# Last batch of a Mamba and mixture-of-experts layer in blocks of 512 tokens, with feed-forward parts spread anew

## The reference

```
h = layernorm(x) * (1 + ca) + sa
x = x + ga * mamba(h)
h = layernorm(x) * (1 + cb) + sb
x = x + gb * ffn(h)

mamba(h):                       # 512 channels, 16 states per channel
    val, gate = split(h @ W_in)
    val = silu(conv3(val))      # along the tokens, centred
    B, C = val @ W_B, val @ W_C
    Delta = softplus((val @ W_delta + delta_base) @ W_tau)
    dA = Delta[..., None] * -exp(A_log)
    A_bar = exp(dA);  B_bar = expm1(dA) / (dA + 1e-6) * Delta * B
    h_t = A_bar_t * h_{t-1} + B_bar_t * val_t          # the scan along 2048 tokens
    y_t = sum over the states of h_t * C_t
    return (y * silu(gate)) @ W_out + h

ffn(h):                         # 8 experts and a shared one, hidden size 256
    scores = sigmoid(h @ gate_W);  the two best experts, weights normalised
    return sum over experts of weight_e * (gelu(h @ W1_e + b1_e) @ W2_e + b2_e)
           + gelu(h @ Ws1 + bs1) @ Ws2 + bs2
```

## Time and profile before

| | |
|---|---|
| median of three runs | 5074.86 us |
| profiled execution | 5076.93 us |
| its span, first to last instruction | 5075.1 us |
| busy: TensorE, VectorE, ScalarE, GpSimd | 3917.0, 4160.2, 3989.1, 3740.0 us |
| mean granted TensorE clock | 0.867 |
| DMA | 1104.28 MB, mean 218 GB/s |

### The profile page before, as it was taken

One profiled execution on the slowest core, in us unless ns is written; L12 is line 12 of the kernel. 1 busy time (PEld: TensorE's weight loads), 2 busy tenths in 40 slices (PEclk: granted clock), 3 DMA queues, 4 the chain that ended last, 5 costly groups with the idle time before them and its releaser, 6 DMA issues.

```text
span 5075.1 us, 36705 instructions
## 1 busy us (share of the span) xinstructions
PE 3917.0 (77%) x9708; PEld 1636.1 (32%) x9708; DVE 4160.2 (82%) x3798; ACT 3989.1 (79%) x4187; POOL 3740.0 (74%) x2292
## 2 busy tenths in 40 slices
PE   6441242888888988888898888898888876778989
PEld 3210010333333333333333333333333323333443
DVE  1277899989899999999898989999999989998110
ACT  2386788898899898988898988889899887887111
POOL 0189997787888887887888887888888797888101
PEclk8775565899999999898999999899999887879989
DMA  4589887788888888888888888888888887777322
GB/s 133 140 270 272 256 232 201 216 237 232 231 257 216 260 237 231 227 234 234 229 240 228 257 217 256 228 242 224 230 255 223 225 226 201 220 206 217 101 91 74
DMA packets 365658, 1104.28 MB, mean 218 GB/s; under 512 B 42501, under 2 KB 45445, under 8 KB 358150
## 3 DMA queue, kind: packets, MB, share of 16 engines
q1 hardware_dynamic: 274314, 799.91, 45.7%
q0 software_dynamic: 91136, 302.03, 30.9%
HBM read 673.29 MB, written 160.06 MB: 164 GB/s over the span
## 4 chain that ended last, share of the span: by engine, by line
PE 17%; issue 17%; ACT 17%; DMA 17%; POOL 16%; DVE 13%; SPq 0%; POOLq 0%; DVEq 0%; ACTq 0%
DMA ysum<-hs 12%; PE ps L1024 5%; PE ps L1040 5%; POOL inv L1302 4%; POOL hs L1279 4%; ACT inv L680 3%; DVE ps L1072 3%; DVE ps L1078 3%; PE ps L994 2%; DVE ps L1085 2%; ACT inv L675 2%; POOL ysum L1289 2%; ACT th L687 1%; ACT inv L685 1%; POOL hid L1319 1%
## 5 line engine op out<-in xcount | busy, mean ns | idle before, releaser
L1302 POOL TENSOR_TENSOR inv<-inv,th 128x1024 f32<-128x1024 f32 x512 | 1279.0, 2498 | 263.7 <-ACT th L687 262.9
L1279 POOL TENSOR_TENSOR hs<-hs,Cb 128x1024 f32<-128x1024 f32 x512 | 1296.7, 2533 | 91.8 <-DVE hs L1102 69.9
L1024 PE MATMUL ps<-hf,w1r 128*128 128x512 f32 x2304 | 1139.8, 649 | 55.0 <-ACT xn L760 30.4
L1051 PE MATMUL ps<-Brow,pick 48*128 48x512 bf16 x1024 | 355.1, 431 | 780.9 <-DVE hs L1102 776.1
L1040 PE MATMUL ps<-w2r,hid 128*128 128x512 f32 x1792 | 833.5, 612 | 1.1 <-issue 1.1
L687 ACT ACTIVATE th<-delta,halfA 128x1024 f32<-128x1024 f32 x512 | 582.7, 1138 | 231.4 <-POOL inv L1302 231.1
L1072 DVE TENSOR_TENSOR ps<-ps,us 128x1024 f32<-128x1024 f32 x512 | 627.7, 1226 | 116.9 <-PE ps L1051 116.6
L1289 POOL DMA_DIRECT2D ysum<-hs x480 | 446.8, 931 | 328.1 <-DMA ysum<-hs 290.5
L1085 DVE SCALAR_TENSOR_TENSOR ps<-ps,coef,inv 128x1024 f32<-128x1024 f32 x512 | 658.2, 1286 | 31.6 <-POOL inv L1302 9.7
L1024 PEld LDWEIGHTS ps<-hf,w1r 128*128 128x128 f32 x2304 | 463.2, 208 | 654.9 <-issue 596.9
L1092 DVE SCALAR_TENSOR_TENSOR ps<-nrd,inv_kappa,ps 128x1024 f32<-128x1024 f32 x512 | 659.0, 1287 | 15.0
(11 more groups left out here) (157 smaller groups left out, 5139.8 us busy)
## 6 DMA issues: line engine op xcount, KB each, us to landing
Cb<-c_rows SPq DMA_DIRECT2D x512, 512.0 KB, 4.7
ysum<-hs POOLq DMA_DIRECT2D x512, 512.0 KB, 5.6
w2r<-w_scaled SPq DMA_DIRECT2D x144, 512.0 KB, 7.0
w1r<-in_W SPq DMA_DIRECT2D x144, 512.0 KB, 6.0
gbc<-expert_gates SPq DMA_DIRECT2D x128, 256.0 KB, 5.5
aw<-in_W_val SPq DMA_DIRECT2D x64, 256.0 KB, 5.1
xa<-in_x SPq DMA_DIRECT2D x32, 512.0 KB, 6.3
h_residual<-hT SPq DMA_DIRECT2D x16, 1024.0 KB, 7.3
```

The source lines that it names most:

```text
L1024: mm = t.matmul(o, w1r[:, n % 2, k, h * P:(h + 1) * P], hf[:, k, :], start=(k == 0), stop=(k == G - 1))
L1279: gp_.tensor_tensor(hs[:, c % 3, :], hs[:, c % 3, :], Cb[:, c % 2, :], ALU.mult).then_inc(hC_done, 1)
L1302: gp_.tensor_tensor(inv[:, c % 6, :], inv[:, c % 6, :], th[:, c % 2, :], ALU.mult).then_inc(thinv_done, 1)
```

## The change

For the first three batches nothing changes but the layout in DRAM. For the last batch a unit is now two channel groups side by side over 512 tokens, 2 x 512 columns, so that a block of 512 tokens takes two units; y of block 12 is whole after unit 25, of 13 after unit 27, of 14 after unit 29, of 15 after unit 31. Instructions that take a constant of the channel are issued once for each half (`for cols, g in parts(u)`): Square, Tanh, the second Exp, times_weight, times_ratio, the scan, and the Ln of inverse_delta.

Slots and steps are taken apart. PACE maps slots to steps: up to slot 383 one step to a slot as before; slots 384 to 511 take the 160 steps of windows 12 to 16; slots 512 to 575 those of windows 17 and 18. ScalarE's places are mapped in the same proportion by share_act. All rows in DRAM lie by blocks of 512. In SyncE's order, the DMAs of the scan (C, unit, u, B, y) stand ahead of the steps' and the gate load and a block's first unit load behind them.

```
-    NK = NQ // 2
-    NU = NK * G
+    NU = NQ * G // 2
...
-    c_d = dram("c_rows", [NK, N, TB])
-    delta_d = dram("delta_rows", [NK, G, P, TB])
+    c_d = dram("c_rows", [NQ, N, T])
+    delta_d = dram("delta_rows", [NQ, G, P, T])
...
+        SIZES = [2] * 6 + [1] * 4
...
+        def rows_of(d, u):
+            (q, n), i = BLOCKS[BLOCK_OF[u]], u - FIRST_U[BLOCK_OF[u]]
+            return (d[q:q + 2, i] if n == 2 else d[q, 2 * i:2 * i + 2]).rearrange("h p t -> p h t")
+
+        def parts(u):
+            n, i = BLOCKS[BLOCK_OF[u]][1], u - FIRST_U[BLOCK_OF[u]]
+            return [(slice(0, TB), i)] if n == 2 else [(slice(0, T), 2 * i), (slice(T, TB), 2 * i + 1)]
...
+        PACE = [(-3 * WIN, 0, -3 * WIN, 0), (0, 2 * WIN, 0, 2 * WIN), (2 * WIN, (NQ - 4) * WIN, 2 * WIN, (NQ - 4) * WIN), ((NQ - 4) * WIN, NQ * WIN, (NQ - 4) * WIN, (NQ + 1) * WIN), (NQ * WIN, (NQ + 2) * WIN, (NQ + 1) * WIN, (NQ + 3) * WIN)]
+        SLOTS = range(PACE[0][0], PACE[-1][1])
+
+        def share(t):
+            for t0, t1, v0, v1 in PACE:
+                if t0 <= t < t1:
+                    j, n, m = t - t0, t1 - t0, v1 - v0
+                    return range(v0 + j * m // n, v0 + (j + 1) * m // n)
...
-                sp.wait_ge(gy_st, 16 * G * (k + 1))
+                sp.wait_ge(gy_st, 16 * units_before_end(qf))
...
+                row = c_d[q:q + 2, n, :] if fronts(u) == q + 2 else c_d[q, n:n + 1, :].broadcast_to([2, T])
+                sp.dma_start(halves(Cb[:, (c + 1) % 2, :]), row.partition_broadcast(P)).then_inc(C_ld[(c + 1) % 2], 16)
...
-                s.activation(th[:, c % 2, :], delta[:, u % 2, :], ACT.Tanh,
-                             scale=halfA[:, c % N, u % G:u % G + 1]).then_inc(th_done, 1)
+                for cols, g in parts(u):
+                    ins = s.activation(th[:, c % 2, cols], delta[:, u % 2, cols], ACT.Tanh, scale=halfA[:, c % N, g:g + 1])
+                ins.then_inc(th_done, 1)
...
+                for cols, g in parts(u):
+                    ins = v.tensor_tensor_scan(hs[:, c % 3, cols], abar[:, c % 4, cols], X(c)[:, cols],
+                                               0.0 if begins(u) else carry[:, g, c % N:c % N + 1], ALU.mult, ALU.add)
+                ins.then_inc(scan_done, 1)
+
+            times_weight(c)
+            for H, r in steps_of(c)[:1]:
+                dve_steps(dve, H, r, True)
+            times_ratio(c)
+            times_u(c + 1)
+            scan(c)
+            times_abar(c + 1)
+            for i, (H, r) in enumerate(steps_of(c)):
+                if i:
+                    dve_steps(dve, H, r, True)
+                dve_steps(dve, H, r)
...
-                for H in WINDOWS:
-                    for r in range(WIN):
-                        pe_slot(pe, H, r)
+                for t in SLOTS:
+                    pe_slot(pe, t)
+                    for H, r in steps_of(t):
+                        pe_steps(pe, H, r)
```

More of the change, by code:

```diff
@@ new lines, in at @@
+            def at(place):
+                if batch % 4 == 1 and place in ("logs", 0):
+                    inverse_delta(4 * batch // N + 1, place)
+                for i in share_act(NP * batch + PLACES.index(place)):
+                    b, j = divmod(i, NP)
+                    act_steps(act, *divmod(b, WIN // 4), PLACES[j])
+            at("start")
+            for c in states[0:2]:
+                square(c)
+            at("half squared")
+            for c in states[2:4]:
+                square(c)
@@ L883, in pe_jobs @@
+            if w == 7:
+                if place == "start":
+                    take_t(qn, (2, 3))
+                    gelu(qf, 2)
         def pe_jobs(H, r):
```

572 lines of the change are left out of this document (306 added, 266 removed).

## The result

| | before | after |
|---|---|---|
| median | 5075.2 us (5061.0 to 5090.0, 4 runs) | 5204.0 us (5194.5 to 5210.4, 4 runs) |
| ratio, 95% interval | | 1.0252 (1.0219 to 1.0285) |
| profiled execution, span | 5076.9, 5075.1 us | 5194.5, 5192.6 us |
| first scan to scan of state 384 | 3343.5 us | 3457.8 us (+114.3) |
| from there to the end of the last scan | 1054.8 us | 1235.4 us (+180.6) |

The account below looks back on a forecast made before the run. VectorE was taken to bound the slots and TensorE alone the stretch behind the last scan. 5075.1 + 145.7 (last 128 slots) - 176.1 (behind them) = 5044.7, forecast as 5045 us, range 4970 to 5105.

Parts of the forecast that it names:

- Behind the last scan: Stretch after the last scan: only block 15's feed-forward part is left there, 390.0 to 213.9 us, a term of -176.1.
- (a), the pieces: DRAM rows by 512 tokens, loads in 2 KB instead of 4 KB pieces: taken as nothing, at most 10 us over the run.
- (b), SyncE's order: SyncE's reordered DMA queue: each DMA waits for things done a window earlier, the C load has a slot of slack; nothing.
- The last 128 slots: From scan 384 to the last: 1054.8 us plus part, cuts and TensorE waits becomes 1200.5, a term of +145.7.
- The cuts: Three VectorE instructions per state halved in the last 128 slots, 384 more: 45 us, bounds 0 to 77.
- The fifth part: One more feed-forward part in the last 128 slots: 14 us of VectorE work and 87 of further waits.
- the dearer bound: VectorE's wait for B in the last 128 slots: 133 us if each TensorE product is 5% longer; 110 was taken.
- Where the lateness stands: 21 of 32 double slots have too much TensorE work; named: 491, 411, 403, 415, 423, 475, 499 and 503.
- The clock: TensorE's granted clock in the last 128 slots: near 0.94, as in window 12 before, keeping waits near the lower price.
- Rival 3: Hand-overs between ScalarE and TensorE come late, 80 us on top of 1200 in the last 128 slots: 5125; chance 0.13.
- Rival 2: Time lost in the last 128 slots, 1256 us and more, eats the 176 gained: 5075 to 5100; chance 0.18.
- marks set for "wrong": Halved pair over 0.2 us dearer, VectorE waiting over 10 us for ScalarE or GpSimd, first 384 slots over 3640 us.

Follow-up runs that it names:

- b_c2k: The kernel before with only the rows of C in DRAM by 512 tokens (2 KB pieces): 5190.0 us, 1.0222.
- b_lnwait: The kernel before with only a block's first load of delta moved to the end of step 19 and waiting for both halves of the log's sum: 5116.5 us, 1.0088.
- a_cuts: a_4k_ln with one step to a slot, halved instructions kept, block 14's part behind the last scan again: 5125.7 us, 1.0094.
- a_4k_ln: The changed kernel with 4 KB rows for blocks 0 to 11 and each load of delta waiting only for the half it reads: 5085.6 us, 1.0030.
- a_bal2_c1: a_c1 with double slots light for TensorE and not close together between a load's issue and its use: 5044.9 us, 0.9944.
- a_c1: a_4k_ln with C loaded once per short block and multiplied into both halves: 5068.3 us, 0.9989.

## Why the prediction was wrong, by its steps

**Behind the last scan: right.** -176.1 said, -178.6 measured.

**"Edits at nothing", (a), the pieces: this step failed.** It had 0 to 10 us for the whole run, from the loads of x (6.3 us, pieces of 2 KB) beside those of w1 (6.0). b_c2k measured +115. The two rows were wrong neighbours: they are of 32 and 144 issues, beside the 512 of C, and a landing time shows what one load costs its own reader, not what it takes from the others. The column that bore on it was left unread: the DMA share of 0.75 to 0.85 in the earlier trace rows, next to 65,536 more packets. The step also looked at the wrong reader, GpSimd's wait for C; the sum of y, on the same DMA engines, was the one that came late. It said that a lost cover "would show as longer waits for the sum of y", and those came, with 74 us instead of 10, though GpSimd waits for no load of C in b_c2k.

**"Edits at nothing", (b), SyncE's order: this step failed too.** "Each waits for things done a window earlier" was not so for st_ln[1], whose sum is issued in step 20 while the wait stands in step 19. The queue behind it was named correctly (the load of C), but the slot of slack that C has is not enough for 18 us, and the load of x behind it was not named. Alone it costs 35 us of slots (b_lnwait, 1.0088), beside the pieces 12 to 21.

**The last 128 slots: the mechanism right, the term 35 us too small.** 1200.5 said, 1235.4 measured. The cuts were 10 us cheaper than the 45 taken (a_cuts): +40.7 us of work for 384 more instructions, 0.11 each, and 6 us fewer waits. The estimate by the Trainium skill (VectorE: DVE Perf Modes, the TRN2 errata), 60 us for the cuts, is further off than the trace. The fifth part was 50 dearer (a_4k_ln against a_cuts): 110 us of wait more, where 87 had been taken, another 7 of VectorE's work, and 21 of waits that had no term. The wait for B, 125.1 us in the changed kernel, came near the dearer bound (133), but not for the reason of that bound, longer products: TensorE's work was 1011 us where 1026 had been taken. The list had only products; TensorE's stands, up to 46 of the 110 us by the count above, were not in it.

**Where the lateness stands: half right.** Double slots carry it, as predicted, and slot 411 and 491 are among the long ones (15.6 and 15.8 us). But of the other six that the list named, 415 alone is above 12 us (403: 10.9, 499: 9.4), and the three longest, 395, 399 and 451 with 19.7, 18.9 and 19.4 us, were not named. The list of products doesn't know of evictions, weight loads and normalisations on which the queue stands.

**The clock: wrong.** About 0.94 was expected in the last 128 slots; four windows of 32 slots in the kernel after show

```profile
3745.80:4088.20 342.40, 300.67 (x747) 126.65 (x748) 279.72 (x354) 295.66 (x395) 236.39 (x161) 0.92 0.81 218
4088.20:4394.60 306.40, 238.67 (x610) 103.69 (x608) 266.95 (x337) 260.15 (x341) 232.78 (x162) 0.85 0.77 199
4394.60:4698.40 303.80, 246.99 (x599) 105.56 (x600) 254.68 (x304) 254.07 (x333) 225.28 (x153) 0.87 0.72 194
4698.40:4981.20 282.80, 224.21 (x558) 96.08 (x556) 248.31 (x298) 222.85 (x295) 209.61 (x116) 0.87 0.77 204
```

of which only the first comes near. TensorE is busy for 88% of that one and for 78% to 81% of the others, and slot 399 shows a stand and a low clock together: the granted clock fell to 1.2 GHz within the stand and was back at 2.4 at 3807.2 us, near the end of the slow product.

**The rivals.** Rival 3 (hand-overs between ScalarE and TensorE late) was the only slower one, at 5125. Its mechanism is there, but inside the 1235 us of the slots (15 us of ScalarE's evictions in the kernel after's waits of TensorE, and ScalarE's wait for first products up from 28.1 to 58.5), not on top of 1200 by 80. Rival 2, the gain used up, is what the change without its side effects gives: a_4k_ln at 5085.6 us, within the 5075 to 5100 that the rival had. That its 1240 us are near the rival's 1256 is luck in part: the cuts cost 34.5 where the rival had 77. What made the kernel 2.5% slower was in none of them. Of the marks set for "wrong", one came: the first 384 slots, which were to end before 3640 us and ended at 3746. The halved pairs cost 0.22 us over a whole instruction where each stands alone by its row (2 x 751 against 1286), and 0.13 in sequence. One slip of the forecast's arithmetic changes nothing: 0.17 and two thirds of 0.52 make 0.52, where it has 0.53.

**What stays open.** First, why some packets take so much longer than the typical one that a packet more costs 41 ns, and whether reads, writes or the DMA engines' own handling are the cause. Second, the make-up of the 151 us: VectorE's own work is 21, and 20 go with the places of double slots (a_bal2_c1 against a_c1); of the rest the runs say that no one engine's sum of work sets it, and the division into stands and products is a count, not an experiment that takes the stands alone away. The 18 us that C loaded twice costs are spread over both the cuts and the part. More buffers for w1 and w2, or more PSUM banks for the products, weren't tried.

## What to carry to other kernels

A change of layout in DRAM that halves a contiguous piece is no detail when the load is repeated hundreds of times: count its packets beside the DMA engines' busy share, try it alone in the old kernel, and look for the victim among the other DMAs, not only at the load's own reader. For every wait that moves in an ordered queue, find the very instruction that signals it and compare the steps in which the two are issued. And where more work is put between two urgent instructions of an ordered queue, the stands inside it (evictions, weight loads) count beside the work, up to 55 and 72 us here.

## What the runs showed of the hardware

- The same 512 KB broadcast from DRAM to 128 partitions lands in 4.7 us in pieces of 4 KB, in 6.4 in pieces of 2 KB and in 10.2 in pieces of 1 KB, under this kernel's load; the kernel's ratio is 1, 1.0222 and 1.1531. Loads that weren't changed go from 6.0 and 7.0 us to 11.7 and 12.0 at the last step.
- With the DMA engines' busy share at 0.83 to 0.85 the kernel's DMA throughput varied between 233 and 199 GB/s: that share did not tell how much was moved.
- The median 2 KB packet of SyncE's queue took 84 ns and the mean one 111 (b_c2k), the median 1 KB packet 46 and the mean one 94 (b_c1k): the smaller the pieces, the more of the time lies in packets slower than the typical one.
- Two half scans cost hardly more than a whole one: on VectorE in order of time, in the kernel after,

```profile
3887.23 2.32 DVE L1189 TENSOR_TENSOR_SCAN hs<-abar,ps 128x512 f32<-128x512 f32 x2
...
3890.78 1.42 DVE L1169 SCALAR_TENSOR_TENSOR ps<-ps,coef,inv 128x512 f32<-128x512 f32 x2
```

the pair of scans takes 2.32 us beside 2.28 for a whole, the pair with the column constant 1.42 beside 1.29.
- On ScalarE a half pass takes 708 ns and a whole one 1138, which alone would make a cut cost 0.28 us. But neighbours overlap: the 250 half passes of the row above are 165.1 us of busy time where 250 x 0.708 would be 177, 1.32 a pair, so in sequence a cut costs 0.18. The sums agree: 906.4 to 976.6 us for 382 more instructions (a_cuts), 0.18 each, where the forecast had 0.21.
